# Turning the normalised rows of a token tower by VectorE and DRAM instead of TensorE

## The reference

```python
h = take(weight, ids) * take(keep_mask, ids)
# part 1, on n = layernorm(h)
x_and_res = n @ in_proj_w.T                 # 256 -> 512 + 256
u, res = x_and_res[..., :512], x_and_res[..., 512:]
u = causal_depthwise_conv(u, 4 taps) + conv_b
delta = softplus(u @ dt_proj_w.T + dt_proj_b)
g = u * sigmoid(delta)
ys = scan(state = 0.9 * state + 0.1 * g)    # along the sequence
h = h + ys @ out_proj_w.T + res
# part 2, on layernorm(h), rows and weights quantised in blocks of 32 to fp6 and back
h = h + dequant(quant(layernorm(h))) @ dequant(quant(ffn_weight)).T + ffn_bias
```

## Time and profile before

| | |
|---|---|
| median of 3 runs | 1011.38 us (1007.56 to 1011.82) |
| the profiled execution's own time | 1011.74 us |
| its span, first to last instruction | 1009.9 us |
| mean granted TensorE clock | 0.988 |
| busy share of the span: TensorE, VectorE, GpSimd, ScalarE | 96%, 85%, 74%, 58% |
| a step of the loop, first matmul to first matmul | 29.83 us |

### The profile page before, as it was taken

How to read it: one execution, slowest core, us unless ns; L and a number is a source line. 1 busy time by engine, 2 the same in 40 slices (tenths; PEclk the granted TensorE clock), 3 DMA queues, 4 the chain that set the end, 5 groups by cost and what they waited for, 6 DMA issues and landing times.

```text
span 1009.9 us, 15142 instructions
## 1 busy us (share of the span) xinstructions
PE 970.3 (96%) x5140; PEld 822.0 (81%) x5140; DVE 854.6 (85%) x1563; ACT 582.3 (58%) x966; POOL 743.1 (74%) x586
## 2 busy tenths in 40 slices
PE   3699999999999999999999999999999999999996
PEld 2477888888888888888888888888888888888885
DVE  4868988888988898888888898889888888889866
ACT  4455665565566565566556556656556655655441
POOL 5657777788777788777778877778877777886661
PEclk9799999999999999999999999999999999999997
DMA  4002122222211222211222221122221122221111
GB/s 152 22 21 63 55 56 80 83 64 85 76 55 56 83 62 83 83 55 54 78 83 62 83 77 55 55 83 62 83 83 53 56 78 83 63 84 64 42 43 42
DMA packets 51468, 68.28 MB, mean 68 GB/s; under 512 B 10096, under 2 KB 42736, under 8 KB 51440
## 3 DMA queue, kind: packets, MB, share of 16 engines
q1 hardware_dynamic: 45296, 51.08, 16.0%
q0 software_dynamic: 6144, 16.85, 6.4%
HBM read 35.40 MB, written 32.51 MB: 67 GB/s over the span
## 4 chain that ended last, share of the span: by engine, by line
PE 93%; DVE 4%; POOL 1%; ACT 1%; DMA 1%; issue 1%; DVEq 0%; POOLq 0%
PE psZ L991 12%; PE psZ L992 12%; PE psZ L998 12%; PE psT L949 6%; PE psT L945 6%; PE psT L946 6%; PE psU L934 6%; PE psU L930 6%; PE psU L931 6%; PE psO L1035 3%; PE psO L980 3%; PE psO L981 3%; PE psO L1036 3%; PE psO L982 3%; PE psO L1037 3%; PE psT L1049 3%
## 5 line engine op out<-in xcount | busy, mean ns | idle before, releaser
L356 POOL TENSOR_TENSOR g_lo<-g,g_hi 128x512 fp32r<-128x512 f32 x128 | 194.5, 1530 | 168.1 <-ACT g_hi L484 168.1
L683 DVE SCALAR_TENSOR_TENSOR u<-psU,cw,u 128x511 f32<-128x511 f32 x378 | 265.0, 743 | 18.6 <-ACT u L466 14.2
L991 PE MATMUL psZ<-u_hi,dt_hi 128*128 128x512 f32 x512 | 206.6, 404 | 10.3 <-ACT u_hi L473 7.1
L998 PE MATMUL psZ<-u_lo,dt_hi 128*128 128x512 f32 x512 | 204.1, 399 | 0.1
L992 PE MATMUL psZ<-u_hi,dt_lo 128*128 128x512 f32 x512 | 203.8, 398 | 0.0
L363 POOL TENSOR_TENSOR u_lo<-u,u_hi 128x512 fp32r<-128x512 f32 x128 | 163.3, 1299 | 15.3 <-ACT u_hi L473 14.0
L466 ACT ACTIVATE u<-psU,cb,cw 128x512 f32<-128x512 f32 x126 | 98.1, 779 | 121.8 <-PE psU L934 115.0
L477 ACT ACTIVATE psZ<-psZ,gate_b 128x512 f32<-128x512 f32 x128 | 84.5, 661 | 113.7 <-PE psZ L998 113.0
L341 POOL DMA_INDIRECT rows<-table,ids x128 | 126.3, 986 | 30.7 <-issue 29.4
L473 ACT ACTIVATE u_hi<-u 128x512 fp32r<-128x512 f32 x128 | 80.5, 629 | 91.9 <-DVE u L683 91.9
L767 DVE SCALAR_TENSOR_TENSOR g<-psZ,u 128x512 f32<-128x512 f32 x128 | 85.4, 687 | 45.6 <-ACT psZ L477 45.6
(11 more groups left out here) (107 smaller groups left out, 2186.7 us busy)
## 6 DMA issues: line engine op xcount, KB each, us to landing
out<-h SPq DMA_DIRECT2D x31, 512.0 KB, 2.9
turned<-xb SPq DMA_DIRECT2D x30, 512.0 KB, 2.8
xT<-turned SPq DMA_DIRECT2D x120, 128.0 KB, 3.5
rows<-table,ids POOLq DMA_INDIRECT x128, 2.9
dt_stage<-dt_wT SPq DMA_DIRECT2D x1, 1024.0 KB, 5.6
g<-in_wT SPq DMA_DIRECT2D x1, 768.0 KB, 4.6
ids<-x SPq DMA_DIRECT2D x32, 2.0 KB, 3.7
ow_stage<-out_wT SPq DMA_DIRECT2D x1, 512.0 KB, 7.4
```

What stands on the lines that cost most here:

```text
L356: pool.tensor_tensor(g_lo[:, m, :], g[:, m, :], f32(g_hi[:, m, :]), ALU.subtract).then_inc(g_lo_ready[m], 1)
L683: dve.scalar_tensor_tensor(u[:, m, back:T], u_psum_tile(st, m)[:, 0:T - back], cw[:, m, TAPS - 1 - back:TAPS - back], u[:, m, back:T], ALU ...
L991: pe.matmul(psZ[:, m % 2, :], dt_hi[:, k, o], u_hi[:, k, :], start=(k == 0), stop=False)
L998: ins = pe.matmul(psZ[:, m % 2, :], dt_hi[:, k, o], u_lo[:, k, :], start=False, stop=(k == M - 1))
```

## The change

The rows of sequence s+1 take the road of the second part's rows, with a DRAM buffer `turned_n` and tiles `nb_blocks` and `nT` of their own:

- TensorE: `transpose_n1` is left out of every step; only the lead-in, which prepares sequence 0, keeps it.
- ScalarE: `normalise1` writes in block order; `split_nT` copies the high part from `nT` in SBUF once the transfers have landed. `first_tap(1)` now stands ahead of `split_g(3)`, and `split_xT` ahead of `split_u(3)`.
- VectorE: `turn_n1` (a block transpose of 128x1024) stands after the taps of channels 0 and 1; `split_nT` is left out of the steps. `turn_blocks` moves up behind `dequantise`; `gate(3)` moves from the end of the step to the next step's start, behind `turn_blocks`; the quantisation moves ahead of `gate(2)`. The taps of channels 0 and 1 alternate.
- SyncE: in each step behind the trip of `xb`, one write, a wait and four reads more.
- GpSimd: `split_nT` (the low part, 128x1024) stands between `inverse_root2` and `g_lo` 0.

The core of the diff:

```diff
+        nb_blocks, nT = sb("nb_blocks", [P, C * D]), sb("nT", [P, C * D])
+        turned_n = nc.dram_tensor("turned_n", (P, C * D), F32, kind="Internal").ap()
...
@@ SyncE, step, between the trip of xb and the load of ids
+                if st.front:
+                    sp.wait_ge(nT_lo_ready, s + 1)
+                    sp.wait_ge(n_turned, s + 1)
+                    sp.dma_start(turned_n, nb_blocks[:]).then_inc(n_written, 16)
+                    sp.wait_ge(n_written, 16 * (s + 1))
+                    for q in range(Q):
+                        blocks = turned_n.rearrange("(a j) (q n) -> q j a n", a=Q, q=Q)[q]
+                        sp.dma_start(nT[q * BLOCK:(q + 1) * BLOCK, :].rearrange("j (a n) -> j a n", a=Q),
+                                     blocks).then_inc(nT_loaded, 16)
...
@@ GpSimd
+                def split_nT():
+                    pool.wait_ge(nT_hi_ready, s + 2)
+                    pool.tensor_tensor(by_token(nT_lo[:, st.nb]), nT_by_token, f32(by_token(nT_hi[:, st.nb])),
+                                       ALU.subtract).then_inc(nT_lo_ready, 1)
...
                 if st.back:
-                    for part in st.back_parts:
-                        inverse_root2(part)
+                    inverse_root2(None)
+                if st.main and st.front:
+                    split_nT()
                 if st.main:
                     split_g(0, s)
...
@@ ScalarE
-                    if later(s + 1):
-                        act.wait_ge(t1_psum, s + 1)
+                    if st.first:
+                        act.wait_ge(t1_psum, 1)
+                    elif st is not lead_in:
+                        act.wait_ge(n_turned, s)
...
+                    act.wait_ge(nT_loaded, Q * 16 * (s + 1))
                     if later(s):
                         act.wait_ge(m_psum[1], s)
-                    act.activation(nT_hi[:, nb], psT[:], ACT.Copy).then_inc(nT_hi_ready, 1)
+                    act.activation(by_token(nT_hi[:, nb]), nT_by_token, ACT.Copy).then_inc(nT_hi_ready, 1)
...
                 first_tap(0)
+                first_tap(1)
                 if st.back:
                     split_g(M - 1, s - 1)
-                first_tap(1)
...
                 split_u(2)
-                split_u(3)
                 if st.tail:
                     split_xT()
+                split_u(3)
...
@@ VectorE
+                def turn_n1():
+
+                    dve.wait_ge(n1_ready, s + 2)
+                    if later(s):
+                        dve.wait_ge(n_written, 16 * s)
+                    dve.transpose(nb_blocks[:], flat(n1[:])).then_inc(n_turned, 1)
...
                 if st.tail:
                     dequantise(None, own=False)
-                convolve(0, 0, 1, 0, 1, 1)
-                if st.tail:
                     turn_blocks()
+                if st.back:
+                    gate(M - 1, s - 1)
+                convolve(0, 1, 0, 1, 0, 1)
+                if st.front:
+                    turn_n1()
...
                 gate(1)
-                if st.front:
-                    split_nT()
                 if st.tail:
                     add_linear(None)
                 if st.back:
                     block_max(None)
-                gate(2)
-                if st.back:
                     quantise()
                     dve.wait_ge(q_ready, s)
-                gate(3)
+                gate(2)
...
@@ TensorE, step
-                if st.front:
-                    transpose_n1()
```

More of the change, by code:

```diff
@@ L192, in lm_tower_kernel @@
         turned_written, xT_loaded = sem("turned_written"), sem("xT_loaded")
+        n_turned, n_written, nT_loaded = (sem(n) for n in ("n_turned", "n_written", "nT_loaded"))
         xT_hi_ready, xT_lo_ready = sem("xT_hi_ready"), sem("xT_lo_ready")
@@ L376, in inverse_root2 @@
                     pool.wait_ge(var2_ready, s + (part or 0))
+                    if later(s - 1):
+                        pool.wait_ge(n2_ready, s - 1)
                     pool.tensor_tensor(rstd2[:, cs], ve2[:, cs], neg_half[:, cs],
@@ L387, in add_bias @@
                                            ALU.add).then_inc(bias_added, 1)
+                def split_nT():
+                    pool.wait_ge(nT_hi_ready, s + 2)
+                    pool.tensor_tensor(by_token(nT_lo[:, st.nb]), nT_by_token, f32(by_token(nT_hi[:, st.nb])),
+                                       ALU.subtract).then_inc(nT_lo_ready, 1)
                 def split_xT():
                     pool.wait_ge(xT_hi_ready, s - 1)
-                    pool.tensor_tensor(by_token(xT_lo), xT_by_token, f32(by_token(xT_hi)),
+                    pool.tensor_tensor(by_token(xT_lo[:]), xT_by_token, f32(by_token(xT_hi[:])),
                                        ALU.subtract).then_inc(xT_lo_ready, 1)
@@ L500, in normalise1 @@
                     act.wait_ge(nmr1_ready, s + 2)
-                    if later(s + 1):
-                        act.wait_ge(t1_psum, s + 1)
+                    if st.first:
+                        act.wait_ge(t1_psum, 1)
+                    elif st is not lead_in:
+                        act.wait_ge(n_turned, s)
                     for c in range(C):
-                        ins = act.activation(n1[:, c, :], h[:, ring, c, :], ACT.Identity, bias=nmr1[:, c:c + 1],
+                        to, h_c = n1[:, c, :], h[:, ring, c, :]
+                        if st is not lead_in:
+                            to, h_c = n1_blocks[:, :, :, c, :], h_c.rearrange("p (k q j) -> p k q j", k=KD, q=Q)
+                        ins = act.activation(to, h_c, ACT.Identity, bias=nmr1[:, c:c + 1],
                                              scale=rstd1[:, c:c + 1])
@@ L538, in split_nT @@
                 def split_nT():
-                    act.wait_ge(t1_psum, s + 2)
+                    if st is lead_in:
+                        act.wait_ge(t1_psum, 1)
+                        act.activation(nT_hi[:, nb], psT[:], ACT.Copy).then_inc(nT_hi_ready, 1)
+                        return
+                    act.wait_ge(nT_loaded, Q * 16 * (s + 1))
                     if later(s):
                         act.wait_ge(m_psum[1], s)
-                    act.activation(nT_hi[:, nb], psT[:], ACT.Copy).then_inc(nT_hi_ready, 1)
+                    act.activation(by_token(nT_hi[:, nb]), nT_by_token, ACT.Copy).then_inc(nT_hi_ready, 1)
                 if st is lead_in:
@@ L761, in add_linear, with gate @@
                                       ALU.add).then_inc(result_ready, 1)
-                def gate(m):
+                def gate(m, s=s):
                     dve.wait_ge(tanh_ready[m], s + 1)
@@ L837, in turn_blocks @@
                     dve.transpose(xb[:], flat(xd[:])).then_inc(xb_ready, 1)
+                def turn_n1():
[3 more added lines that the diff above has]
+                    dve.transpose(nb_blocks[:], flat(n1[:])).then_inc(n_turned, 1)
                 def split_nT():
-                    dve.wait_ge(nT_hi_ready, s + 2)
-                    if later(s):
-                        dve.wait_ge(m_psum[1], s)
+                    dve.wait_ge(nT_hi_ready, 1)
                     dve.tensor_tensor(nT_lo[:, nb], psT[:], f32(nT_hi[:, nb]), ALU.subtract).then_inc(nT_lo_ready, 1)
@@ L1059, in transpose_n1 @@
                 def transpose_n1():
-                    if st is not lead_in:
-                        pe.wait_ge(n1_ready, s + 2)
-                    if later(s + 1):
-                        pe.wait_ge(nT_lo_ready, s + 1)
-                    if later(s):
-                        pe.wait_ge(scan_ready[0], s)
-                        pe.wait_ge(scan_ready[1], s)
                     to_channels(lambda c, k: n1[:, c, k * P:(k + 1) * P], psT, t1_psum)
```

6 lines of the change are left out of this document (4 added, 2 removed).

## The result

The changed kernel takes **1040.36 us** (median of 4 runs, 1039.18 to 1041.07); the kernel before, run beside it, 1011.49 us. The ratio is 1.029, with a 95% interval from 1.027 to 1.032. 1037 was forecast, in a range of 1018 to 1056. The profiled execution has a span of 1039.2 us, 29.3 more than before.

A forecast was written before the change was run, and what follows sets the result against it. TensorE's matmuls bound the kernel; the held `nm1` would make the step a 30.71 us closed loop. 24.4 - 0.9 + 1.9 + 0.8 = 26.2 us on 1011.74 gives 1037.9, median 0.4 lower: forecast 1037 us, range 1018 to 1056.

The forecast's parts named there:

- The transposes are worth 0.88 us: TensorE, each step: removing eight transposes saves 0.88 us, giving 28.96 us a step if TensorE stayed the bound.
- `nT_lo` holds `nm1` for 1.87 us: VectorE, each loop step: `nm1` is held until GpSimd's `nT_lo` ends, 1.87 us, delaying `gate(0)` and `dt_proj(2)`.
- The closed loop is 30.71 us: Loop step through `dt_proj(2)`, `g_lo` 3, `xT_lo` and `nT_lo`: 30.71 us against 29.84, 0.87 us more.
- the sum: Durations added around the loop through `dt_proj(2)`: 30.71 us a step, with TensorE waiting 1.75 us.
- The sign "1.5 to 2 us": TensorE's timeline: a wait of 1.5 to 2 us before `dt_proj(2)` in each step, released by VectorE's gate.
- some 50: List of waits: TensorE's wait before `dt_proj(2)` comes to some 50 us in total.
- VectorE's load does not change: VectorE, each step: it gives up `split_nT`, 1.21 us, and takes a second block transpose, 1.23 us.
- the trip costs nothing in the loop: DRAM trip of 8.15 us: costed at nothing, with 0.9 us to spare for ScalarE and 5 us for GpSimd.
- Steps 0 and 1: +0.8 and +1.9: First two steps: the trip delays `tanh(0)` by 0.8 us in step 0; held `nm1` costs 1.9 in step 1.
- a rival for the loop: TensorE's clock falls too after its waits, in every second loop step: 21 us more, 1058 us, chance 0.12.
- The loop's term: Steps 2 to 29: 28 steps at 0.87 us more each, 24.4 us.
- The matmuls stay the bound: Rival for the loop: `nm1` passes before `nT_lo`, so TensorE's matmuls still bound the step; 987 us, chance 0.12.

The follow-up runs named there:

- e1: Changed kernel with one wait more, GpSimd starting `nT_lo` only when VectorE has done `nm1` and `ve1`: 988.3 us, ratio 0.979 to the kernel before.
- e2: Changed kernel with `nT_lo` split into two instructions of 128x512: 1005.8 us, ratio 0.996 to the kernel before.
- e11: Changed kernel with `nm1` and `ve1` written as `tensor_reduce`, nothing moved: 990.4 us, ratio 0.980 to the kernel before.
- e3: Kernel before the change plus one unused 128x1024 subtraction on GpSimd behind `nmr2`: 1028.5 us, ratio 1.018.
- e6: Kernel before the change plus the trip's DRAM transfers alone, on a constant tile nobody uses: 1011.8 us, ratio 1.003.
- e8: e1 with the old instruction order on VectorE and ScalarE: 1036.1 us, ratio 1.027 to the kernel before.

## Why the prediction was right

- *The transposes are worth 0.88 us.* Steps that wait for nothing are 28.93 to 28.95 us (step 30; e1), against 28.96 forecast.
- *`nT_lo` holds `nm1` for 1.87 us.* From `nm1`'s start to `nT_lo`'s end it is 1.91; `nm1` takes 1.94 in all, 1.77 more than by itself. e1, e2 and e11 change that and next to nothing else, e3 puts it into the kernel before, and each time the step follows.
- *The closed loop is 30.71 us.* 30.64. `g_lo` 3 starts 4.37 us into the step (forecast 4.40), `xT_lo` ends at 20.36 (20.36), `linear` starts at 20.50 (20.51). `dt_proj(2)` starts at 24.94 (25.11 by the sum), and from there it is 5.71 us to the next step (5.60). TensorE's wait is 1.41; the 1.75 of the sum counts as 1.59 in a trace, as the prediction says, and 0.11 of the rest is the slower start behind the wait. The sign "1.5 to 2 us" was thus just missed, and the 48.1 us in all fit "some 50" by luck: 8.7 of them are in steps 0 and 1, and the loop has 39.4.
- *VectorE's load does not change; the trip costs nothing in the loop.* `turn_n1` is 1.23 us, e6 has 29.83 us in the loop with the transfers added, and e1's 28.95 leaves the trip no room to cost. VectorE's busy time did rise by 64 us, from 854.6 to 918.9, but by held time: the `tensor_scalar`s that write `nm1` and `nm2` take 76.7 us together instead of 18.8, and `bscale` 15.1 instead of 6.1. And ScalarE's `nT_hi` was in most steps released neither by `merge` nor by the trip: it stood behind the mask of the gathered rows, which waits for them now (27.8 us in the list above; the rows land later, and ScalarE comes to the mask earlier, 16.84 us into the step of the lines above against 17.31).
- *Steps 0 and 1: +0.8 and +1.9.* **This term was mis-sized: +4.1 and +3.3.** For step 0 I counted the trip on its way to `nT_hi`, and missed two things. The trip's transfers make the gathers land later, so that the mask starts 2.0 us later (1.5 to 1.7 in e6, by the transfers alone), and `nm1` is held there too (1.24 us), because GpSimd, waiting for `nT_hi`, starts `nT_lo` 1.13 us before it (45.88). For step 1 the delay of `dt_proj(2)` was right (1.71), and the clock fell behind it (1.56), which I had only as a rival for the loop. The loop's term erred the other way by 1.9 (24.4 against 22.5). So the total, 26.2 forecast and 29.3 measured, is nearer than these two terms are: they partly cancel, which is luck.
- *Rivals.* "The matmuls stay the bound" needed `nT_lo` half a microsecond later or `nm1` earlier: e1 is that kernel, at 988 where 987 was worked out. The clock stayed up in the loop at 1.41 us of idle time per step (PEclk 1.00 in every stretch from 91 to 979 us).

What stays open: what made the clock fall in one of two like cases (below), and what each of the moves that e8 undoes is worth.

## What to carry to other kernels

Before moving work to an idle GpSimd, look at which VectorE instructions will arrive while it runs: a 4-element `tensor_scalar` between two SBUF tiles is held until GpSimd's instruction ends, with all that queues behind it. Three cures were cheap here: let GpSimd start after it, write it as `tensor_reduce`, or put the urgent work ahead of it. And price a new transfer at the first place where another transfer is waited for, not only where its own data are wanted.

## What the runs showed of the hardware

- Held by a running GpSimd subtraction: `tensor_scalar` 128x4 (1.94 for 0.17 us), and `scalar_tensor_tensor` with both inputs in SBUF, 128x4 (1.93) and 128x1024 (1.80 for 1.23). Not held: `tensor_reduce` 128x4 (0.16), and the gates, with an input in PSUM (0.69).
- GpSimd is held in its turn. In the kernel before, its `rstd1` (128x4) begins 0.15 us into VectorE's dequantising, an instruction with both inputs in SBUF, and takes 1.99 us; in the changed kernel, where a gate runs beside it, it takes 1.01 (at 491.91).

```profile
503.19 1.27 DVE L745 SCALAR_TENSOR_TENSOR xd<-q,bscale 128x1024 f32<-128x1024 fp8e4 x1
503.34 1.99 POOL L370 TENSOR_TENSOR rstd<-ve,neg_half 128x4 f32<-128x4 f32 x1
```

- A waiting VectorE instruction gets in between two GpSimd instructions that follow each other without a gap (e2: `nm1` ends at 497.20, the first half at 497.18, the second half at 498.41).
- The same idle time did and did not lower TensorE's clock. In step 1 of e1 (first row, and first window) and of e11 (second ones) it waited 2.18 us before `dt_proj(2)`:

```profile
79.40 0.50 PE L1029 MATMUL psZ<-u_hi,dt_hi 128*128 128x512 f32 x1 [2.18 <-DVE g L800]
```

```profile
80.47 0.50 PE L1028 MATMUL psZ<-u_hi,dt_hi 128*128 128x512 f32 x1 [2.18 <-DVE g L799]
```

```profile
81.00:83.00 2.00, 2.00 (x6) 1.55 (x5) 1.88 (x3) 0.25 (x1) 2.00 (x3) 0.50 0.04 8
```

```profile
81.00:83.00 2.00, 2.00 (x10) 1.59 (x9) 1.66 (x3) 1.33 (x3) 1.61 (x2) 1.00 0.00 0
```

The granted clock was 0.50 (1.2 GHz) in the one and 1.00 (2.4 GHz) in the other, where it stayed at 1.00 until 88.00, and step 1 took 32.36 and 30.80 us. So the length of a wait alone does not tell whether the clock falls.
